# Five of eleven down-projection groups of a decoder layer as bare FP4 codes in two passes, with the running sum rescaled on VectorE

## The chip, the cores and the metric

The kernel runs on one core of one Trainium2 chip. The metric is the time of the program on the device in microseconds (us), as the median of several runs. The core has five engines that run side by side and meet only through semaphores: TensorE (matrix products, PE in the profile, its weight loads PEld), VectorE (DVE), ScalarE (ACT), GpSimd (POOL) and SyncE (SP), which here issues every DMA. Each engine works off its own instructions in order: an instruction that waits holds up all behind it on that engine.

## What is computed

x and ctx are 8 x 256 x 512 in fp32. Three stages, each followed by a layer norm with a residual:

```
x  = LN(x + attention(x))            # linear attention with a memory, head width 128
x  = LN(x + conv(ctx, ctx, x))       # 32 heads of 8: outer products of ctx, causal convolution, times x
x  = LN(x + ffn(x))

def ffn(x):
    w_gu   = FP4_LUT[gate_up codes] * scale    # [2816, 512], a scale for each row and group of 128 inputs
    w_down = FP4_LUT[down codes] * scale       # [512, 1408], 11 groups of 128 inputs, down_scales [11, 512]
    gate, up = split(x @ w_gu.T)
    y = (silu(gate) * up) @ w_down.T
    return y / sqrt(mean(y * y) + 1e-6)
```

## The kernel before

**Stages.** The attention works in 8 slots of 256 tokens; its results x1 go to DRAM in two layouts (x1_rows by token, x1_blocks for the transposed reads). Then come 8 groups g of 256 tokens for convolution and FFN. They are pipelined in passes: pass g does the convolution of group g (c0 to c15 on TensorE, tm0 to tm15 on VectorE, tr0 to tr3 on GpSimd) and the FFN of group f = g - 1. The attention, the unpacking of the weights and pass 1 (its steps bear a "+") share one written-out order, the start. Passes 2 to 7 follow one order (PE_ORDER and its sisters); 3 to 6 are a loop; in pass 7 the steps of the next group are left out. Pass 8 has only FFN (LAST_PE and its sisters). The steps kq, ct, kn, ln, d0 and d1 in a pass belong to the next group. The half t = 1 of the down projection of group f (y1_i) is done in the pass after that of its half t = 0 (y0_i); in the last pass the half t = 1 of the last group is called w1_i.

**What sets the order.** For each engine, an order of step names is written out by hand in the text, and every step waits on semaphores for what it needs. No step moves by itself.

**Gate and up.** w_gu is kept as bare FP4 codes, exact in fp16, for each group of 128 inputs k = 0 to 3. gi_p is phase p of hidden tile i: four matmuls of 256 columns (x2_hi and x2_lo, gate and up) into one bank of p_gu. Between the phases ScalarE multiplies the running sum in place by a ratio of scales (rsi_p, line 1134). Silu (gu on ScalarE), the product (gu on VectorE, line 1201), h_hi (hhi, ScalarE, line 1151) and h_lo (hli, GpSimd, line 1102) follow.

**Down.** y0_i, y1_i and w1_i are down(f, t, i), lines 1290 to 1304. The weight of group i is scaled in fp32 and split into wd_hi + wd_lo in fp16; a step has three matmuls of 512 columns with accumulation over all eleven groups in one PSUM bank p_y[t]: h_hi by wd_hi (line 1297), h_hi by wd_lo (1298), h_lo by wd_hi (1299). Then a square sum (n0, n1 on ScalarE), a mean (a), a root on GpSimd (a, b), the residual z with its statistics (b, line 1216) and the norm to fin (e, line 1232), which SyncE stores. Capitals (A1, B1, E1, N1) are the same steps of the last group's half 1.

**The weights in the start.** Tiles n = 0 to 21 are gate/up, 22 to 32 down. wsn (GpSimd) lays out bytes or multiplies a down tile by its scale, wn (TensorE) flips it, by one 128-column flip for a gate/up tile and four for a down tile; whn (ScalarE) makes the fp16 high part and wln (VectorE, line 795) the low part of the down tiles. u0 to u4 (VectorE) unpack the codes.

**Other steps named below.** Xa, Xb: flips of x; Q, V, S, M, N, T, Oa, Ob: attention products on TensorE; dn, lc, o: denominators, local part and sum of attention; qs, bn, pw, nb, nm: statistics and norm of x1 (nm, ScalarE, line 631). On SyncE, stn stores x1 of slot n (one DMA at line 410, eight at line 415), xn loads x, cx ctx, tw writes the Toeplitz rows, toe reads them, xq and xr read x1_blocks and x1_rows. In the convolution kq (VectorE, line 223) transposes xq, hk and kl/lk/ln split the pair products (pr, pn on GpSimd) into kv_hi (line 180) and kv_lo (line 216), f and ct flip ctx, rt and xt flip the sum and x2; bs, bn, nm and the xt of VectorE (line 285) end in x2_lo, for which the first gate step g0_0 of the next pass waits.

The step on TensorE that changes:

```python
def down(f, t, i):
    ...
    pe.wait_ge(h_low, f * GI + i + 1)
    nc.tensor.matmul(p_y[t][:], h_hi[:, i, c], wd_hi[:, i, :], start=(i == 0), stop=False)
    nc.tensor.matmul(p_y[t][:], h_hi[:, i, c], wd_lo[:, i, :], start=False, stop=False)
    done = nc.tensor.matmul(p_y[t][:], h_lo[:, i, c], wd_hi[:, i, :], start=False, stop=(i == GI - 1))
```

## Time and profile before

| | |
|---|---|
| runs | 536.75, 536.4, 536.91 us; median 536.75 |
| profiled execution: span from first to last instruction | 535.3 us (it has no other time of its own) |
| TensorE busy | 508.7 us, 95% |
| ScalarE | 415.7 us, 78% |
| GpSimd | 394.7 us, 74% |
| VectorE | 374.4 us, 70% |
| mean granted TensorE clock | 0.995 of full |
| DMA | 40.63 MB, mean 76 GB/s |

The start with pass 1 ends at about 180 us; passes 2 to 6 take some 51.2 us each, pass 7 some 46; pass 8 begins near 482. Busy times of TensorE are modelled and overlap (a 512-column matmul is listed with 0.38 us though the next begins 0.22 us later), so its cost is read from one start to the next. A line of the timeline gives the start in us, the duration, the engine, the line of the kernel, the operation, output <- input with their shapes and a count; in square brackets stands the idle time of the engine before it and what ended it.

### The profile page before, as it was taken

Reading aid. Unit: us, or ns where it says so; the run is one execution under the profiler, and the core shown is the slowest. Engines: PE = TensorE matmul, PEld = TensorE weight load, DVE = VectorE, ACT = ScalarE, POOL = GpSimd, SP = SyncE. Lnnn points to the kernel's source line nnn. Section 1 sums busy time; section 2 is a strip of 40 time slices with the busy share of each in tenths; the row PEclk is TensorE's granted clock in tenths of the full one; section 3 lists DMA queues with packets and bytes.
Section 4 is the critical chain, followed back from the end, with each engine's and each line's share of the span. In section 5 each row is a group of like instructions: output and inputs, shape, how many; then the busy total and the mean of one; then the engine's idle time right before and its main releaser. Section 6 shows DMA issues by size and latency. Waiting matters only on the chain.

```text
span 535.3 us, 11768 instructions
## 1 busy us (share of the span) xinstructions
PE 508.7 (95%) x3676; PEld 377.6 (71%) x3676; DVE 374.4 (70%) x1145; ACT 415.7 (78%) x994; POOL 394.7 (74%) x449
## 2 busy tenths in 40 slices
PE   8888899998999999999999999999999999999992
PEld 5676787777785777677767776777677767765660
DVE  2886668988787667776777776768777777763223
ACT  4577875277999788788888897889788877788981
POOL 2768864994898499769968995899589859871231
PEclk9999999999999999999999999999999999999997
DMA  8713776443250862032104210411040111001001
GB/s 224 203 39 63 169 142 180 128 80 99 87 112 24 159 127 86 23 100 79 60 1 117 59 59 0 118 59 59 13 130 14 39 33 49 0 1 42 1 21 39
DMA packets 66146, 40.63 MB, mean 76 GB/s; under 512 B 37882, under 2 KB 55418, under 8 KB 66106
## 3 DMA queue, kind: packets, MB, share of 16 engines
q1 hardware_dynamic: 66106, 40.13, 29.6%
q8 instruction: 20, 0.33, 0.3%
q14 instruction: 20, 0.16, 0.1%
HBM read 27.46 MB, written 12.66 MB: 75 GB/s over the span
## 4 chain that ended last, share of the span: by engine, by line
PE 36%; POOL 27%; issue 19%; ACT 5%; DVE 4%; SPq 4%; DMA 2%; POOLq 1%; DVEq 0%; ACTq 0%
POOL shared L297 9%; POOL h_lo L1102 5%; SPq L415 4%; POOL kv L197 3%; PE p_cv L137 3%; PE p_cv L139 3%; PE p_cv L138 3%; PE p_n L1299 3%; PE p_n L1297 3%; PE p_n L1298 3%; POOL shared L299 2%; PE p_x L1284 2%; PE p_x L1286 2%; PE p_qk L1284 2%; PE p_qk L1286 2%
## 5 line engine op out<-in xcount | busy, mean ns | idle before, releaser
L1102 POOL TENSOR_TENSOR h_lo<-w,h_hi 128x256 f16<-128x256 f32 x88 | 73.6, 842 | 44.6 <-ACT h_hi L1151 43.0
L137 PE MATMUL p_cv<-kv_hi,toe 128*128 128x288 f16 x320 | 91.6, 286 | 1.3 <-DVE shared L257 1.3
L139 PE MATMUL p_cv<-kv_hi,toe 128*128 128x288 f16 x320 | 91.5, 286 | 0.0
L138 PE MATMUL p_cv<-kv_lo,toe 128*128 128x288 f16 x320 | 91.5, 286 | 0.0
L1134 ACT ACTIVATE p_qk<-p_qk,rescale 128x256 f32<-128x256 f32 x192 | 78.3, 451 | 12.5 <-PE p_qk L1286 11.9
L297 POOL TENSOR_TENSOR shared<-shared 128x1024 f32<-128x1024 f32 x32 | 76.8, 2399 | 8.9 <-DVE shared L257 8.8
L1134 ACT ACTIVATE p_x<-p_x,rescale 128x256 f32<-128x256 f32 x192 | 78.4, 452 | 6.2 <-PE p_x L1286 6.0
L1134 ACT ACTIVATE p_s<-p_s,rescale 128x256 f32<-128x256 f32 x144 | 59.0, 456 | 11.2 <-PE p_s L1286 11.1
L1297 PE MATMUL p_n<-wd_hi,h_hi 128*128 128x512 f16 x176 | 66.8, 379 | 0.0
L1298 PE MATMUL p_n<-wd_lo,h_hi 128*128 128x512 f16 x176 | 66.7, 379 | 0.0
L1299 PE MATMUL p_n<-wd_hi,h_lo 128*128 128x512 f16 x176 | 66.7, 379 | 0.0
L1284 PE MATMUL p_qk<-x_hi,wg_hi 128*128 128x256 f16 x256 | 63.0, 273 | 3.6 <-DVE x_lo L285 2.1
L1284 PE MATMUL p_x<-x_hi,wg_hi 128*128 128x256 f16 x256 | 62.9, 273 | 0.7 <-ACT p_x L1134 0.2
L1286 PE MATMUL p_x<-x_lo,wg_hi 128*128 128x256 f16 x256 | 62.8, 273 | 0.0
L1286 PE MATMUL p_qk<-x_lo,wg_hi 128*128 128x256 f16 x256 | 62.8, 273 | 0.0
L239 DVE TENSOR_TENSOR shared<-p_cv,qv 128x128 f32<-128x128 f32 x128 | 36.1, 282 | 32.4 <-PE p_cv L139 31.8
L216 DVE TENSOR_TENSOR kv_lo<-kv,kv_hi 128x1152 f16<-128x1152 f32 x32 | 52.6, 1642 | 3.4 <-ACT kv_hi L180 3.4
L242 DVE TENSOR_TENSOR shared<-p_cv,qv 128x128 f32<-128x128 f32 x128 | 49.7, 388 | 0.0
L299 POOL TENSOR_TENSOR shared<-shared 128x512 f32<-128x512 f32 x32 | 47.7, 1492 | 2.5
L1284 PE MATMUL p_s<-x_hi,wg_hi 128*128 128x256 f16 x192 | 47.1, 273 | 0.9 <-ACT p_s L1134 0.9
L1286 PE MATMUL p_s<-x_lo,wg_hi 128*128 128x256 f16 x192 | 47.1, 273 | 0.0
L180 ACT CAST kv_hi<-kv 128x1152 f16<-128x1152 f32 x32 | 37.3, 1166 | 10.9 <-POOL kv L208 7.2
(170 smaller groups left out, 1270.6 us busy)
## 6 DMA issues: line engine op xcount, KB each, us to landing
toe<-toeplitz_rows SPq DMA_DIRECT2D x16, 512.0 KB, 4.0
cnat<-in_ctx SPq DMA_DIRECT2D x16, 256.0 KB
xq<-x_blocks SPq DMA_DIRECT2D x16, 256.0 KB, 5.7
xr<-x_rows SPq DMA_DIRECT2D x16, 256.0 KB
out_x<-fin SPq DMA_DIRECT2D x16, 256.0 KB
ring<-in_x SPq DMA_DIRECT2D x6, 512.0 KB, 4.4
x_rows<-ring SPq DMA_DIRECT2D x6, 512.0 KB, 2.9
x_blocks<-ring SPq DMA_DIRECT2D x48, 64.0 KB
```

Of the source, the lines that this page charges most:

```text
L137: nc.tensor.matmul(dst, hi, kh, start=(mb == 0), stop=False)
L138: nc.tensor.matmul(dst, hi, kl, start=False, stop=False)
L139: done = nc.tensor.matmul(dst, lo, kh, start=False, stop=(mb == lb))
L297: nc.gpsimd.tensor_tensor(T[:, :, 0:256], T[:, :, 0:256], T[:, :, 256:512], ALU.add).then_inc(cv.tree, 1)
L299: nc.gpsimd.tensor_tensor(T[:, :, 0:128], T[:, :, 0:128], T[:, :, 128:256], ALU.add).then_inc(cv.tree, 1)
L1102: nc.gpsimd.tensor_tensor(h_lo[:, i, :], h32[:, i % 2, :], h_hi[:, i, :], ALU.subtract).then_inc(h_low, 1)
L1134: done = nc.scalar.activation(sums, sums, ACT.Copy, scale=rescale[:, p - 1, part * GI + i:part * GI + i + 1])
L1284: nc.tensor.matmul(dst, whi, cv.x2_hi[:, k, :], start=(k == 0 and part == 0), stop=False, skip_group_check=True)
L1286: done = nc.tensor.matmul(dst, whi, cv.x2_lo[:, k, :], start=False, stop=True, skip_group_check=True)
L1297: nc.tensor.matmul(p_y[t][:], h_hi[:, i, c], wd_hi[:, i, :], start=(i == 0), stop=False)
L1298: nc.tensor.matmul(p_y[t][:], h_hi[:, i, c], wd_lo[:, i, :], start=False, stop=False)
L1299: done = nc.tensor.matmul(p_y[t][:], h_lo[:, i, c], wd_hi[:, i, :], start=False, stop=(i == GI - 1))
```

## The change

EX = 5: the down groups 0 to 4 are kept as bare codes. Their weight tiles are laid out and flipped as gate/up tiles are, there is no wd_lo for them, and down(f, t, i) has two matmuls for i < 5. After each of them VectorE multiplies the running sum in the bank by the ratio of the scales of group i and group i + 1, a row of 512 numbers (rescale_down, steps s0_i, s1_i and, for the last half, S1_i); y_(i+1) waits for that. The remaining weights enter with their scales as before. The bank's ratio of group 4 is the scale itself, since group 5 is not a bare code.

The ratios are made once: SyncE loads the scales of five groups onto 16 partitions, VectorE forms ratios (dr0, five small operations), rw0 stores them to DRAM in runs of 128 bytes, and rl0 loads them onto all 128 partitions (five rows of 2 KB for each, 1.31 MB). The tensor early, which receives them, holds pk_d, kin, kpad and the fp32 scale rows until then. high_h waits for the last reader of its h_hi by another semaphore. deviations (ScalarE) and add_residual (VectorE) get a wait on their own engine's earlier work. All sequences are new.

```diff
+EX = 5
...
+    early = keep["early"]
+    srow_gf = early[0:KD * OG, 1856:1984]
+    srow_df = early[0:GI * 4, 1984:2112]
...
+        sp.dma_start(dn_rows[:], dn_scales[0:EX].rearrange("g (p c) -> p g c", c=32)).then_inc(in_dr, 16)
...
+            elif name == "rw":
+                sp.wait_ge(ratios_made, 5)
+                sp.dma_start(ratio_rows.rearrange("g (p c) -> p g c", c=32), dn_abs[:]).then_inc(ratios_stored, 16)
+            elif name == "rl":
+                sp.wait_ge(ratios_stored, 16)
+                sp.wait_ge(scales_flipped, 2)
+                sp.wait_ge(unpacked, 30)
+                sp.wait_ge(rows_stored, 16)
+                sp.dma_start(early[:, 0:EX * D].rearrange("p (g d) -> p g d", g=EX), bass.AP(ratio_rows.tensor, 0, [[0, P], [D, EX], [1, D]])).then_inc(
+                    keep["in_ratio"], 16)
...
-                if kind == "g":
+                if kind == "g" or idx < EX:
                     out = w32[:, n % 2, 0:P].bitcast(U8).rearrange("p (c h g) -> p h g c", h=2, g=4)
-                    src = vg.bitcast(U8)[:, idx * 256:(idx + 1) * 256].rearrange("p (g c) -> p g c", g=4)
+                    if kind == "g":
+                        src = vg.bitcast(U8)[:, idx * 256:(idx + 1) * 256].rearrange("p (g c) -> p g c", g=4)
+                    else:
+                        src = vd.bitcast(U8).rearrange("p (t g c) -> p g t c", t=4, g=GI)[:, idx]
...
+            elif idx < EX:
+                dst = keep["wd_hi"][:, idx, :].rearrange("p (t c) -> p t c", t=4)
+                src = wbank[n % 2][:, 0:P].bitcast(F8).rearrange("p (c t) -> p t c", t=4)
...
+            wait(act, deviated, 2 * i)
...
+        def down_ratios():
+
+            dve.wait_ge(in_dr, 16)
+            nc.vector.tensor_scalar(dn_abs[:], dn_rows[:], FP4_SHIFT, None, ALU.mult).then_inc(ratios_made, 1)
+            dve.wait_ge(ratios_made, 1)
+            nc.vector.tensor_scalar(dn_rec[:], dn_abs[:], 0.0, NO_SCALE, ALU.is_equal, ALU.mult).then_inc(
+                ratios_made, 1)
+            dve.wait_ge(ratios_made, 2)
+            nc.vector.tensor_tensor(dn_abs[:], dn_abs[:], dn_rec[:], ALU.add).then_inc(ratios_made, 1)
+            dve.wait_ge(ratios_made, 3)
+            nc.vector.reciprocal(dn_rec[:, 1:EX], dn_abs[:, 1:EX]).then_inc(ratios_made, 1)
+            dve.wait_ge(ratios_made, 4)
+            nc.vector.tensor_tensor(dn_abs[:, 0:EX - 1], dn_abs[:, 0:EX - 1], dn_rec[:, 1:EX], ALU.mult).then_inc(
+                ratios_made, 1)
+
...
-            for g in range(1 if n < OG else 4):
+                pe.wait_ge(w_low, n - 2 - OG - EX + 1)
+            for g in range(1 if n < OG + EX else 4):
...
-            if i < GI - 1:
-                wait(act, h_spent, (f - 1) * (GI - 1) + i + 1)
+            if i < EX:
+                wait(act, y_part[1], (f - 1) * EX + i + 1)
+            elif i < GI - 1:
+                wait(act, h_spent, (f - 1) * (GI - 1 - EX) + i - EX + 1)
...
+        def rescale_down(f, t, i):
+            dve.wait_ge(y_part[t], f * EX + i + 1)
+            if isinstance(f, int) and f == 0 and t == 0 and i == 0:
+                dve.wait_ge(keep["in_ratio"], 16)
+            nc.vector.tensor_tensor(p_y[t][:], p_y[t][:], keep["early"][:, i * D:(i + 1) * D], ALU.mult).then_inc(y_rescaled[t], 1)
...
+            wait(dve, fin_made[t], f)
...
+            if 0 < i <= EX:
+                pe.wait_ge(y_rescaled[t], f * EX + i)
+            nc.tensor.matmul(p_y[t][:], h_hi[:, i, c], wd_hi[:, i, :], start=(i == 0), stop=False,
+                             skip_group_check=True)
+            if i >= EX:
+                nc.tensor.matmul(p_y[t][:], h_hi[:, i, c], wd_lo[:, i - EX, :], start=False, stop=False,
+                                 skip_group_check=True)
+            done = nc.tensor.matmul(p_y[t][:], h_lo[:, i, c], wd_hi[:, i, :], start=False,
+                                    stop=(i < EX or i == GI - 1), skip_group_check=True)
+            if i < EX:
+                done.then_inc(y_part[t], 1)
...
-    START_SYNC = ("x3 x4 cx2 st0 cx3 tw0 x5 st1 st2 x6 st3 toe0 xq0 xq2 toe1 xq1 x7 cx5 cx4 xr1 xr0 toe2 st4 cx6 xq3 "
-                  "xr2 toe3 xq5 xr3 st5 toe4 xq4 cx7 st6 toe5 st7").split()
+    START_SYNC = ("x3 tw0 cx2 x4 cx3 rw0 toe0 toe1 st0 x5 st1 st2 x6 st3 rl0 xr1 xq0 cx4 xr0 xq1 x7 cx5 xq2 "
+                  "xq3 toe3 toe2 xq5 xr2 xq4 xr3 toe4 st4 cx7 toe5 cx6 st5 st6 st7").split()
-    START_DVE = ("ze0 is0 u0 sg0 mk0 ig0 dn0 fs0 o0 u1 sg1 ra0 rb0 bm0 mk1 u2 dn1 bn0 o1 kl0 nb0 sg2 ra1 rb1 bm1 mk2 "
...
-                 "wl23 o4 wl24 wl25 wl26 ra4 rb4 wl27 sg5 bm4 wl28 mk5 wl29 wl30 dn5 bn4 wl31 o5 wl32 kq0 tm0 tm1 sg6 "
-                 "tm2 tm3 nb4 tm4 kl2 tm5 kq1 tm6 ra5 tm7 rb5 tm8 mk6 tm9 kl3 tm10 tm11 dn6 tm12 tm13 o6 tm14 tm15 bm5 "
...
+    START_DVE = ("ze0 is0 sg0 ig0 mk0 u0 dn0 o0 u1 sg1 ra0 rb0 bm0 mk1 u2 dn1 bn0 o1 sk0 ra1 sg2 rb1 bm1 mk2 "
...
+                 "mk4 nb3 dn4 o4 kl0 ra4 rb4 sg5 wl27 wl28 wl29 wl30 mk5 wl31 wl32 bm4 kq0 dn5 kl1 tm0 tm1 "
+                 "tm2 o5 tm3 tm4 kq1 tm5 kl2 tm6 sg6 ra5 tm7 tm8 rb5 tm9 tm10 kq2 kl3 mk6 tm11 bm5 tm12 tm13 "
...
-    START_ACT = ("xa0 kw0 kw1 xb0 kw2 kw3 re0 ge0 vk0 ks0 xa1 xb1 lc0 rv0 wh0 wh1 re1 ok0 kt0 wh2 rv1 wh3 qs0 xa2 vk1 "
-                 "xb2 wh4 hk0 wh5 lc1 re2 ok1 wh6 nm0 wh7 wh8 qs1 xa3 vk2 xb3 wh9 hk1 lc2 wh10 ok2 wh11 re3 wh12 wh13 "
-                 "qs2 xa4 vk3 wh14 xb4 nm1 lc3 wh15 wh16 wh17 wh18 ok3 nm2 wh19 re4 wh20 qs3 vk4 wh21 xa5 wh22 xb5 nm3 "
...
+    START_ACT = ("xa0 xb0 kw0 kw1 kw2 kw3 re0 ge0 vk0 xa1 xb1 lc0 ks0 ok0 re1 wh0 wh1 rv0 wh2 wh3 rv1 kt0 "
+                 "xa2 vk1 qs0 xb2 kt1 wh4 wh5 lc1 ok1 re2 wh6 wh7 wh8 wh9 hk0 xa3 vk2 wh10 xb3 wh11 qs1 lc2 "
+                 "rv2 nm0 ok2 re3 wh12 wh13 wh14 wh15 qs2 xa4 vk3 wh16 xb4 nm1 lc3 wh17 wh18 ok3 re4 wh19 "
...
-    START_PE = ("ze0 Xa0 iw0 iw1 iw2 Xb0 iw3 Q0 iz0 V0 S0 Xa1 M0 N0 Xb1 w0 w1 Q1 T0 w2 f0 w3 Oa0 Ob0 Xa2 S1 V1 w4 w5 "
...
-                "Xb4 w15 M3 N3 w16 Q4 w17 T3 w18 f1 Oa3 w19 Ob3 w20 w21 Xa5 V4 S4 M4 w22 w23 Xb5 N4 w24 Q5 T4 w25 w26 "
-                "Oa4 Ob4 w27 w28 Xa6 V5 w29 S5 w30 Xb6 M5 N5 w31 w32 Q6 c0 c1 c2 c3 c4 f2 T5 Oa5 c5 S6 c6 c7 c8 Ob5 "
-                "f3 c9 Xa7 V6 c10 c11 M6 N6 Xb7 c12 rt0 c13 c14 c15 T6 Q7 Oa6 Ob6 +c0 +c1 rt1 S7 V7 xt0 M7 N7 xt1 "
...
+    START_PE = ("ze0 Xa0 Xb0 iw0 iw1 iw2 iw3 Q0 V0 S0 Xa1 M0 N0 Xb1 iz0 Q1 T0 w0 w1 Xa2 Oa0 Ob0 w2 S1 f0 w3 "
...
+                "w13 Oa2 Ob2 w14 w15 V3 S3 w16 w17 Xb4 M3 N3 w18 Q4 T3 f2 w19 w20 Oa3 Ob3 w21 Xa5 V4 S4 w22 "
+                "Xb5 M4 N4 w23 w24 Q5 T4 w25 w26 Oa4 Ob4 w27 w28 V5 w29 w30 Xa6 S5 w31 M5 w32 N5 Xb6 c0 c1 "
+                "Q6 c2 c3 c4 Xa7 T5 c5 c6 Oa5 f3 c7 c8 Ob5 S6 c9 c10 V6 c11 c12 M6 N6 c13 Xb7 c14 c15 rt0 T6 "
...
-    PE_ORDER = ("y1_0 g0_0 g1_0 y1_1 g0_1 y1_2 ct0 g1_1 g0_2 y1_3 y1_4 g2_0 g0_3 c2 g1_2 g3_0 c3 y1_5 g2_1 g1_3 g3_1 "
-                "c4 g2_2 c5 y1_6 g4_0 g2_3 c6 g3_2 c7 g4_1 g5_0 y1_7 g3_3 c8 g5_1 c9 y1_8 g4_2 y1_9 g5_2 c10 g6_0 "
-                "y1_10 c11 g4_3 g6_1 g5_3 ct1 c12 g7_0 g6_2 c13 c14 g8_0 g7_1 c15 y0_0 g7_2 g8_1 g6_3 rt0 y0_1 g7_3 "
-                "g8_2 y0_2 g9_0 y0_3 g10_0 g8_3 g9_1 y0_4 g10_1 g9_2 d0 rt1 y0_5 g10_2 g9_3 y0_6 d1 g10_3 xt0 y0_7 "
-                "y0_8 y0_9 xt1 y0_10").split()
+    PE_ORDER = ("g0_0 g1_0 y1_0 g2_0 g0_1 ct0 g1_1 g2_1 g0_2 g1_2 g0_3 y1_1 g1_3 c2 g3_0 c3 g3_1 g4_0 y1_2 "
+                "g2_2 c4 g3_2 g4_1 c5 g2_3 c6 y1_3 c7 g5_0 y1_4 y0_0 g3_3 g5_1 y1_5 g4_2 ct1 c8 g5_2 y1_6 "
+                "y1_7 g4_3 y1_8 y1_9 g6_0 y1_10 c9 c10 g5_3 g7_0 c11 c12 g6_1 g7_1 c13 g8_0 g6_2 g7_2 c14 "
+                "c15 g8_1 y0_1 g6_3 g7_3 g8_2 y0_2 rt0 g9_0 g10_0 y0_3 g8_3 g9_1 g10_1 y0_4 rt1 g9_2 g10_2 "
+                "y0_5 g9_3 g10_3 xt0 y0_6 y0_7 y0_8 xt1 y0_9 y0_10 d0 d1").split()
-    DVE_ORDER = ("tm0 tm1 gu0 lk1 tm2 tm3 gu1 tm4 tm5 gu2 lk2 tm6 tm7 tm8 gu3 tm9 tm10 lk3 tm11 gu4 a1 tm12 gu5 tm13 "
-                 "kq0 tm14 tm15 b1 gu6 gu7 ln kq1 bs0 bn0 bs1 bn1 gu8 nm0 gu9 nm1 gu10 xt0 xt1 a0 b0 e1 e0").split()
+    DVE_ORDER = ("s1_0 tm0 gu0 tm1 lk1 gu1 s1_1 tm2 tm3 s1_2 tm4 tm5 s1_3 gu2 lk2 s1_4 tm6 tm7 tm8 gu3 lk3 "
+                 "gu4 a1 tm9 tm10 s0_0 gu5 tm11 tm12 tm13 b1 tm14 tm15 s0_1 gu6 gu7 s0_2 bs0 s0_3 bn0 s0_4 "
+                 "bs1 nm0 gu8 bn1 gu9 gu10 xt0 nm1 ln xt1 e1 a0 b0 kq0 kq1 e0").split()
-    LAST_PE = ("y1_0 y1_1 y1_2 g0_0 g1_0 g2_0 g0_1 g1_1 y1_3 y1_4 g0_2 g2_1 g1_2 y1_5 g0_3 g2_2 g1_3 y1_6 g3_0 g2_3 "
-               "g4_0 g3_1 y1_7 g5_0 y1_8 g4_1 y1_9 g3_2 y0_0 g5_1 g4_2 y1_10 g3_3 g5_2 y0_1 g4_3 y0_2 g6_0 g5_3 g6_1 "
-               "g7_0 y0_3 g6_2 g8_0 g7_1 g6_3 y0_4 g7_2 w1_0 g8_1 g9_0 w1_1 g7_3 y0_5 w1_2 g10_0 g8_2 w1_3 g9_1 "
-               "g10_1 g8_3 g9_2 w1_4 g10_2 w1_5 g9_3 w1_6 g10_3 w1_7 y0_6 w1_8 w1_9 w1_10 y0_7 y0_8 y0_9 y0_10").split()
+    LAST_PE = ("g0_0 g1_0 g2_0 y1_0 g0_1 g1_1 g2_1 g0_2 g1_2 g2_2 y1_1 g0_3 g1_3 g2_3 y1_2 g3_0 g4_0 y1_3 "
+               "g3_1 y0_0 g4_1 y1_4 g5_0 g3_2 g4_2 y1_5 y1_6 g5_1 g3_3 g4_3 y1_7 y1_8 g6_0 g7_0 y1_9 y1_10 "
+               "g6_1 g7_1 y0_1 g5_2 g6_2 g7_2 w1_0 g5_3 g6_3 g7_3 y0_2 w1_1 g8_0 g9_0 y0_3 w1_2 g10_0 g8_1 "
+               "g9_1 w1_3 g10_1 y0_4 g8_2 w1_4 g9_2 g10_2 g8_3 w1_5 g9_3 w1_6 g10_3 y0_5 w1_7 w1_8 w1_9 "
+               "w1_10 y0_6 y0_7 y0_8 y0_9 y0_10").split()
-    LAST_DVE = ("gu0 gu1 gu2 a1 gu3 gu4 gu5 b1 gu6 gu7 gu8 e1 gu9 gu10 A1 B1 a0 b0 E1 e0").split()
+    LAST_DVE = ("s1_0 s1_1 gu0 gu1 s1_2 s1_3 gu2 s1_4 s0_0 gu3 gu4 a1 s0_1 b1 S1_0 gu5 gu6 s0_2 S1_1 gu7 "
+                "S1_2 s0_3 S1_3 S1_4 e1 s0_4 gu8 gu9 gu10 A1 B1 a0 b0 E1 e0").split()
...
```

## Rows read from the trace of the kernel before

**Rows 1.** Windows view: window, its length, busy us (xcount) per engine, PEclk.
```profile
119.50:180.00 60.50, 57.27 (x434) 42.83 (x435) 47.69 (x142) 54.07 (x129) 44.51 (x49) 1.00 0.37 84
...
282.30:333.50 51.20, 51.02 (x389) 37.71 (x387) 38.47 (x122) 42.89 (x105) 42.90 (x46) 1.00 0.22 61
...
482.00:510.00 28.00, 26.66 (x187) 17.54 (x186) 8.95 (x20) 25.41 (x71) 5.66 (x9) 1.00 0.07 20
```

**Rows 2.** Waits of the pass 282.3 to 333.5: total us, times, longest.
```profile
DVE shared L239 <- PE p_cv L139: 4.5, 5, 1.4
...
PE p_qk L1284 <- DVE x_lo L285: 0.2, 1, 0.2
```

**Rows 3.** The chain that ended last, shares by engine (page).
```profile
PE 36%; POOL 27%; issue 19%; ACT 5%; DVE 4%; SPq 4%; DMA 2%; POOLq 1%; DVEq 0%; ACTq 0%
```

**Rows 4.** Timeline of TensorE, pass 4: start, us, instruction.
```profile
320.16 0.38 PE L1297 MATMUL p_n<-wd_hi,h_hi 128*128 128x512 f16 x1
...
320.81 0.27 PE L1284 MATMUL p_x<-x_hi,wg_hi 128*128 128x256 f16 x1
...
321.68 0.29 PE L137 MATMUL p_cv<-kv_hi,toe 128*128 128x288 f16 x1
...
322.05 0.60 PE L102 MATMUL p_ct<-ident,shared 128*128 128x128 f32 x4
322.49 0.38 PE L1297 MATMUL p_n<-wd_hi,h_hi 128*128 128x512 f16 x1
```

**Rows 5.** Groups by line, VectorE: busy us, mean ns, idle before.
```profile
L285 DVE TENSOR_TENSOR x_lo<-p_ct,x_hi 128x512 f16<-128x512 f32 x16 | 11.0, 690 | 12.8 <-ACT x_hi L184 12.7
...
L265 DVE TENSOR_TENSOR shared<-p_ct,xr 128x512 f32<-128x512 f32 x16 | 10.7, 671 | 4.5 <-PE p_ct L102 4.5
```

**Rows 6.** Timelines of VectorE and GpSimd in the same pass.
```profile
287.00 1.36 DVE L216 TENSOR_TENSOR kv_lo<-kv,kv_hi 128x1152 f16<-128x1152 f32 x1 [0.58 <-ACT kv_hi L180]
...
327.31 0.69 DVE L285 TENSOR_TENSOR x_lo<-p_ct,x_hi 128x512 f16<-128x512 f32 x1 [0.22 <-ACT x_hi L184]
...
287.36 1.54 POOL L1102 TENSOR_TENSOR h_lo<-w,h_hi 128x256 f16<-128x256 f32 x1 [1.64 <-ACT h_hi L1151]
...
326.87 1.46 POOL L1102 TENSOR_TENSOR h_lo<-w,h_hi 128x256 f16<-128x256 f32 x2 [0.45 <-ACT h_hi L1151]
```

**Rows 7.** Timelines at the pass boundary: TensorE once, then VectorE.
```profile
328.25 0.60 PE L102 MATMUL p_ct<-ident,shared 128*128 128x128 f32 x4
...
282.92 1.40 DVE L1232 TENSOR_SCALAR fin<-z,mv,rs 128x512 f32<-128x512 f32 x1 [0.53 <-POOL rs L1098]
...
329.51 0.69 DVE L285 TENSOR_TENSOR x_lo<-p_ct,x_hi 128x512 f16<-128x512 f32 x1 [1.50 <-ACT x_hi L184]
...
331.07 0.75 DVE L1216 SCALAR_TENSOR_TENSOR z<-p_n,rr,x2hold 128x512 f32<-128x512 f32 x1 [0.66 <-POOL rr L1098]
...
332.93 0.15 DVE L1224 TENSOR_SCALAR ve<-mv 128x1 f32<-128x1 f32 x1
```

**Rows 8.** Timelines in the start: VectorE (kq0), TensorE (c2).
```profile
87.06 0.71 DVE L223 STREAM_TRANSPOSE qv<-xq 128x512 f32<-128x512 f32 x1 [1.14 <-DMA xq<-x_blocks]
...
88.92 0.30 PE L137 MATMUL p_cv<-kv_hi,toe 128*128 128x288 f16 x1 [0.65 <-DVE shared L257]
```

**Rows 9.** Timelines in the start: DMA issues of SyncE, then ScalarE (lc2).
```profile
38.37 7.19 SPq L415 DMA_DIRECT2D x_blocks<-ring  x8
...
56.44 0.38 SPq L410 DMA_DIRECT2D x_rows<-ring  x1
...
72.21 8.19 SPq L415 DMA_DIRECT2D x_blocks<-z  x8
...
83.34 4.90 SPq L426 DMA_DIRECT2D xq<-x_blocks  x2
...
44.94 0.64 ACT L600 ACTIVATE loc<-p_n,coef 128x128 f32<-128x128 f32 x2
```

**Rows 10.** DMA view, 78 to 92 us: GB/s in 40 equal slices.
```profile
GB/s 86 87 87 85 86 84 88 87 82 75 89 106 302 246 222 252 249 184 67 173 294 174 23 20 6 0 0 0 0 0 0 91 94 328 356 376 380 348 301 244
```

More of the change, by code:

```diff
@@ L811, in step @@
                 factor_scales()
+            elif name == "dr":
+                down_ratios()
             elif name == "sk":
@@ L1037, in periods @@
         "y_done", "y_squared", "y_used", "rr_made", "rs3_made", "fin_made", "y_steps"))
+    y_part, y_rescaled = ([sem(f"{n}{t}") for t in range(GT)] for n in ("y_part", "y_rescaled"))
     def before(i):
@@ L1296, in down @@
             pe.wait_ge(h_low, f * GI + i + 1)
[L1297 to L1300 removed]
+            if 0 < i <= EX:
[9 more added lines that the diff above has]
+                done.then_inc(y_part[t], 1)
+            elif i == GI - 1:
                 done.then_inc(y_done[t], 1)
@@ new lines, in decoder_layer @@
+    START_SYNC = ("x3 tw0 cx2 x4 cx3 rw0 toe0 toe1 st0 x5 st1 st2 x6 st3 rl0 xr1 xq0 cx4 xr0 xq1 x7 cx5 xq2 "
+                  "xq3 toe3 toe2 xq5 xr2 xq4 xr3 toe4 st4 cx7 toe5 cx6 st5 st6 st7").split()
+    START_PE = ("ze0 Xa0 Xb0 iw0 iw1 iw2 iw3 Q0 V0 S0 Xa1 M0 N0 Xb1 iz0 Q1 T0 w0 w1 Xa2 Oa0 Ob0 w2 S1 f0 w3 "
[9 rows of a table added]
+                "+y0_6 +y0_7 +y0_8 +y0_9 +xt1 +y0_10 +d0 +d1").split()
+    START_DVE = ("ze0 is0 sg0 ig0 mk0 u0 dn0 o0 u1 sg1 ra0 rb0 bm0 mk1 u2 dn1 bn0 o1 sk0 ra1 sg2 rb1 bm1 mk2 "
[7 rows of a table added]
+                 "+kq0 +b0 +kq1 +e0").split()
@@ new lines, in decoder_layer @@
+    ACT_ORDER = ("rv0 rs0_1 rs1_1 rs2_1 rs0_2 rs1_2 rs0_3 rs1_3 tl gu0 hk1 gu1 hh0 rs3_1 rs2_2 rs3_2 rs4_1 "
+                 "hh1 rs2_3 hk2 rs4_2 rs3_3 ct0 gu2 rs5_1 rv1 rs5_2 gu3 hh2 rs4_3 hh3 hk3 gu4 ho0 rs5_3 n1 "
+                 "rs6_1 hh4 gu5 rs7_1 rs6_2 hh5 rs7_2 rs8_1 ct1 rs6_3 rs7_3 ho1 rs8_2 gu6 gu7 hh6 rs8_3 hh7 "
+                 "rs9_1 rs10_1 gu8 rs9_2 rs10_2 rs9_3 rs10_3 hh8 gu9 gu10 xt0 hh9 hh10 kn xt1 n0").split()
+    POOL_ORDER = ("pr1 pr2 hl0 hl1 tr0 pr3 hl2 tr1 hl3 pn a1 hl4 hl5 tr2 tr3 bn0 hl6 b1 hl7 hl8 bn1 hl9 hl10 "
+                  "a0 b0").split()
```

61 lines of the change are left out of this document (28 added, 33 removed), and 36 rows, old and new, of tables (START_ACT, START_DVE, START_PE, START_POOL).

## The prediction

> **What bounds the kernel now.** I read the windows view first. In a steady pass of 51.20 us TensorE is busy 51.02 us, ScalarE 42.89, GpSimd 42.90, VectorE 38.47, at full granted clock [rows 1]. The waits of that pass agree: TensorE waits only 0.2 us, for the low half of x2, while VectorE waits 4.5 us for convolution sums [rows 2]. The chain of waits credits GpSimd with 27% [rows 3], but a step followed back through an engine that sits idle in between is no proof that it binds; here TensorE has no gap. What a pass costs is its matmuls' start-to-start time: three of 512 columns take 0.65 us (0.217 each), one gate/up step 0.44, three of 288 columns 0.37, four flips of 128 columns 0.44 [rows 4]. Ahead of pass 2 TensorE is less full: it idles 3.2 of 60.5 us from 119.5 to 180 [rows 1], and the start waits for memory once (below). In the last pass TensorE is busy 26.66 and ScalarE 25.41 of 28 us: both nearly bind [rows 1].
>
> **What is removed.** 8 FFN passes x 2 token halves x 5 groups = 80 matmuls of 512 columns: 80 x 0.217 = 17.3 us of TensorE. They are spread as 5 in pass 1 (only y0), 10 in each of passes 2 to 7, 15 in the last (y1, y0, w1). Weights 22 to 26 need one flip instead of four: 15 x 0.11 = 1.65 us of TensorE in the start, and five residuals of 0.69 us on VectorE go (the shape of L285) [rows 4, 5].
>
> **What is added on VectorE.** 80 multiplies of a 128x512 PSUM bank by SBUF ratios. The nearest rows are L265 (671 ns) and L285 (690 ns), both PSUM with SBUF [rows 5]. No row writes PSUM from VectorE; I take 0.67, bounds 0.6 and 0.9. Ten a pass make 6.7 us: VectorE rises to 45.2 of a pass that could be 51.2 - 2.17 = 49.0 us, so its unfilled time must shrink from 12.7 to 3.8 us. GpSimd: when both inputs of a VectorE operation lie in SBUF the two exclude each other: the h_lo at 287.36 takes 1.54 us beside L216, but two beside L285 (PSUM and SBUF) take 1.46 together [rows 6]. So I charge the multiplies nothing on GpSimd; were they to hold it up by all of their 6.7 us, GpSimd would need 42.9 + 6.7 = 49.6 us, above 49.0. The Trainium skill's "SBUF — State Buffer", in its section on the two separate sides, says the pair of ports is an exclusive lock, taken by VectorE operations with two SBUF inputs against GpSimd operations that read SBUF. By that page too the new multiply, with one SBUF input, takes no lock; by the trace's lock row alone 49.6 us would have stood.
>
> **The new chain.** y_i, multiply, y_(i+1) is serial: a multiply (0.67) plus two hand-overs, about 0.9 us. In the steady orders the links of y0_1 to y0_5 have 1.3 us of other TensorE work between, so they hold if VectorE is free. The weak link is at the pass boundary. Call X the end of the second x_lo. Before: X = 329.51 + 0.69 = 330.20, z starts 0.87 later, ve ends 2.9 later (332.93 + 0.15), and the second fin takes 1.40 us beside GpSimd's pair products [rows 7]. The new VectorE order is xt1, e1, a0, b0, kq0, kq1, e0, then s1_0. e1 delays a0 by 0.5, so ve ends at X + 3.4; two transposes of 0.7 [rows 8] bring X + 4.7; e0 (0.7, as the other 128x512 operations, to 1.4) and s1_0 (0.67) give X + 6.1 to 6.8. On TensorE y0_9, y0_10 (1.3) and d0, d1 (1.1) follow the flips xt1. Before, x_lo ended 1.95 us after those flips began (328.25) [rows 7]; now ln stands before it, so 1.95 to 2.4. TensorE reaches g0_0 at 0.44 + 2.4 = 2.84 after the flips began: X + 0.4 to 0.9. From there to y1_1 its order holds nine gate steps (4.0), y1_0 (0.43) and ct0 (0.44): 4.8 us. y1_1 wants to start at X + 5.2 to 5.7 and may at X + 6.1 to 6.8: 0.4 to 1.6 us of stall; I take 1.2, since e0 again meets the pair products. Net of the 2.17 us removed: 1.0 us gained a pass (bounds 0.4 and 1.9), six passes: -6.0. The new self-waits (ScalarE's on deviated, VectorE's on fin_made) stand behind work long done in order: nothing; if they cost, 0.2 us at 8 and 16 places.
>
> **The start.** SyncE's queue. Before, st0 issues from 38.37 (7.19 us), st1 from 56.44, st3's blocks from 72.21 (8.19 us), and xq0 at 83.34 once they landed [rows 9]. kq0 waits 1.14 us for it and TensorE reaches c2 at 88.92 after 0.65 us [rows 8]. Two things delay xq0. First, nm0, which releases st0, now stands behind lc2 on ScalarE; that ran at 44.94 [rows 9], so st0 issues at about 47 instead of 38, ends near 55, and x5, which waits for its landing (3 us), holds back st1 to about 58.5: +0 to +2.3. Second, rl0 (128 x 10 KB = 1.31 MB) and xr1 (0.26 MB) are issued before xq0. The transfers of that stretch peaked at 380 GB/s and ran at about 250 with toe0 [rows 10]: 1.57 MB are 4.1 to 6.3 us, of which toe0 (0.52 MB, 2.1 us), now loaded early, is given back: +0 to +4.2, less where st3 is waited for. I take 90.5 for kq0 (87.1 to 93.5). Behind kq0 in VectorE's order stand dn5, kl1 (1.36, its shape in [rows 6]) and only then tm0: c2 at about 94.0 against 88.92, +5.1. The 1.65 us of flips vanish in that wait; c0, c1 moved ahead of Q6 only fill it. Given back behind it: 5 matmuls (1.1), the context flip f2 that moved ahead (0.4), and of the 3.2 us idle [rows 1] I take 1.5. Start: +2.1 (bounds -2.7, no wait, and +5.5). The Trainium skill, "DMA: Bandwidth & Descriptors", section "Queues, rings and completion order", says that an engine consumes the descriptors of one queue in ring order; by it xq0 cannot pass rl0, and the upper bound of +4.2 would hold. No row here shows two such loads queued.
>
> **The last pass.** 15 x 0.217 = 3.25 us less on TensorE. ScalarE's rescales stay; it starts some 2 us earlier, since three gate steps now lead, but g10_3 soon waits for it, and s1_0, s1_1 precede gu0. I take -2.0 (bounds -1.0 and -3.3).
>
> **Sum.** 2.1 - 6.0 - 2.0 = -5.9. The profiled span is 535.3, the median of the three runs 536.75 (the profiled execution has no time of its own beside its span): about 1.45 us lie around the span, and I leave them as they are. 536.75 - 5.9 = 530.8 us.
>
> **Rivals.**
> (A) The order hides everything: no stall at the boundary, none in the start: 17.3 + 1.65 off, 517.8 us. For it: the tight boundary of before costs only 0.2 us. Against: the 3.8 us that VectorE has left. Chance 0.17.
> (B) The start alone costs more: xq0 behind rl0 comes 6 us later than I take, with x7 and Xa7 behind it; the passes gain as forecast: 536.8 us. Chance 0.15.
> (C) Slower: VectorE becomes the bound. Its work is 45.2 us; before, it waited 12.7 us a pass in order. As soon as more than 6.0 of these remain, a pass is longer than 51.2. With 7.0 it is 52.2: six passes +6.0, start +2.1, last pass -2.0: 542.9 us. For it: in-order waits for TensorE's double-buffered convolution banks (4.5 us) come from TensorE's order, which the multiplies don't change. Against: TensorE's shorter order makes those inputs come earlier. Chance 0.18.
> A fourth, that the two-pass groups save no matmul time, has no ground: the 0.217 us are per matmul, whatever its operand.
>
> **How the numbers follow.** My forecast, 530.8, has 0.50 with a range of its own of 525 to 535. (A) 0.17, (B) 0.15, (C) 0.18. A tenth left out at each end gives 521 to 540. A measurement tells about 0.2% (1.1 us): faster is below 535.7, slower above 537.8. The forecast and (A) are faster (0.67); (B) straddles: 0.05 faster, 0.06 same, 0.04 slower; (C) slower 0.17, same 0.01. Faster 0.72, same 0.07, slower 0.21.
>
> **What would show it.** Matmuls of 512 columns: 448 instead of 528. A steady pass of 50.2 us (A: 49.0; C: over 51.2). In the boundary, a TensorE wait for the multiply of about 1.2 us, once a pass, ahead of y1_1. Multiplies of 0.67 us; h_lo on GpSimd no longer beside them. kq0 waiting 5 us or more for xq in the start, c2 near 94. Wrong would be: multiplies over 0.9 us, TensorE waits spread over all links (C), or an xq0 that lands before 87 (A).

## The result, and the profile of the changed kernel

The changed kernel takes 539.88 us (median of 6 runs, 537.92 to 541.01) against 536.83 (median of 6, 536.40 to 537.69) for the kernel before: a ratio of 1.0051, with a 95% interval of 1.0034 to 1.0069. It is slower by about 0.5%. The forecast was 530.8; the time lies just inside the range's upper end of 540, on the wrong side of zero. The profiled execution of the changed kernel took 537.92 us, with a span of 536.2; its other runs lie up to 3.1 us above it, and I come back to that.

First the three windows that answer to [rows 1] and to a stretch of the start: the start behind the first query blocks, a steady pass, the last pass (window, length, busy us per engine in the order TensorE, weight loads, VectorE, ScalarE, GpSimd, then the granted clock, the DMA share and GB/s).

```profile
90.00:120.00 30.00, 21.97 (x158) 16.93 (x159) 23.05 (x94) 7.28 (x13) 19.03 (x19) 0.83 0.33 88
...
284.86:335.48 50.62, 50.07 (x378) 36.20 (x376) 42.54 (x131) 42.66 (x106) 40.82 (x46) 1.00 0.21 62
482.00:510.00 28.00, 27.00 (x181) 16.15 (x180) 14.79 (x30) 24.97 (x69) 7.18 (x12) 1.00 0.08 20
```

Two things are to be seen. A steady pass is 50.62 us, 0.58 shorter than the 51.20 of [rows 1], although 2.17 us of matmuls left it. And from 90 to 120 TensorE is busy 22 of 30 us, at a granted clock of 0.83. The same stretch of the kernel before:

```profile
90.00:120.00 30.00, 28.56 (x202) 22.04 (x201) 26.88 (x100) 14.04 (x25) 26.63 (x22) 1.00 0.51 134
```

The waits behind it stand in the timelines of VectorE and TensorE. These rows answer to [rows 8], and then come the next convolutions (start, us, instruction, idle before and its releaser).

```profile
94.58 0.71 DVE L224 STREAM_TRANSPOSE qv<-xq 128x512 f32<-128x512 f32 x1 [10.73 <-DMA xq<-x_blocks]
...
95.73 1.35 DVE L217 TENSOR_TENSOR kv_lo<-kv,kv_hi 128x1152 f16<-128x1152 f32 x1
97.00 0.28 DVE L240 TENSOR_TENSOR shared<-p_cv,qv 128x128 f32<-128x128 f32 x1
```
```profile
98.00 0.42 PE L138 MATMUL p_cv<-kv_hi,toe 128*128 128x288 f16 x1 [9.71 <-DVE shared L258]
98.22 0.45 PE L139 MATMUL p_cv<-kv_lo,toe 128*128 128x288 f16 x1
...
101.46 0.29 PE L138 MATMUL p_cv<-kv_hi,toe 128*128 128x288 f16 x1
101.58 0.29 PE L139 MATMUL p_cv<-kv_lo,toe 128*128 128x288 f16 x1
```

kq0 starts 7.5 us later than before, c2 9.1 us later, and from c2 to 101.4 the 288-column matmuls follow one another every 0.24 us, afterwards every 0.12. TensorE had idled 9.7 us, and its clock stood at the lower of its two levels (1.2 GHz) when it came back. SyncE's issues answer to [rows 9]:

```profile
48.11 6.55 SPq L421 DMA_DIRECT2D x_blocks<-ring  x8
...
57.87 0.47 SPq L416 DMA_DIRECT2D x_rows<-ring  x1
...
75.46 8.40 SPq L421 DMA_DIRECT2D x_blocks<-z  x8
84.04 0.60 SPq L478 DMA_DIRECT2D early<-ratio_rows  x1
85.24 0.66 SPq L436 DMA_DIRECT2D xr<-x_rows  x1
86.66 0.39 SPq L432 DMA_DIRECT2D xq<-x_blocks  x1
```

xq0 is issued at 86.66 instead of 83.34 (+3.3 us) and kq0 starts 7.92 us after that issue instead of 3.72 (+4.2). kl1 (1.35 us) and the denominators now stand between kq0 and tm0: from kq0 to c2 it is 3.42 us instead of 1.86 (+1.6). 3.3 + 4.2 + 1.6 = 9.1.

A ledger of the two profiled executions needs points that mean the same in both. I take the start of a pass as its first gate matmul, less the down matmuls ahead of it in the order (one y1 of 0.65 us in a steady pass of the kernel before, three in its last, none in the changed kernel).

| stretch | before | after | difference | forecast |
|---|---|---|---|---|
| start with pass 1 | 176.10 | 183.81 | +7.71 | +2.1 |
| passes 2 to 7 | 305.81 | 302.05 | -3.76 | -6.0 |
| last pass, to the end of the span | 53.39 | 50.34 | -3.05 | -2.0 |
| sum, the span | 535.30 | 536.20 | +0.90 | -5.9 |

Counted like this, pass 7 of the kernel before takes 49.9 us, not the 46 named ahead of the prediction, and the start ends at 176.1, not at 180.

The start can be split at c2. It comes 9.1 us later. From c2 to pass 2 the changed kernel needs 1.4 us less (85.8 instead of 87.2), although 3.4 us of that stretch ran at half the rate, which costs some 1.7. So 1.7 + 1.4 = 3.1 us were given back there, as the forecast has it (3.0 in its sum); how this divides among its three parts was not measured.

### The profile page after: what moved, and what is told of

It reads as the page before. It is cut to its first block, busy times and chain, and to the rows that moved or that the text cites. A ratio compares the mean times of both kernels' runs of the same rounds, so it can differ in the third digit from the quotient of the medians.

```text
span 536.2 us, 11775 instructions
## 1 busy us (share of the span) xinstructions
PE 501.7 (94%) x3581; PEld 364.4 (68%) x3581; DVE 407.9 (76%) x1225; ACT 412.5 (77%) x994; POOL 377.5 (70%) x449
## 4 chain that ended last, share of the span: by engine, by line
PE 30%; POOL 24%; issue 16%; ACT 13%; DVE 7%; SPq 6%; DMA 3%; POOLq 1%; ACTq 0%; DVEq 0%
POOL shared L298 7%; SPq L421 5%; POOL h_lo L1145 4%; ACT p_x L1177 3%; PE p_cv L138 3%; ACT p_qk L1177 3%; PE p_cv L139 3%; PE p_cv L140 3%; PE p_n L1353 3%; PE p_n L1358 3%; POOL kv L198 2%; POOL kv L203 2%; POOL shared L305 2%; ACT p_s L1177 2%; PE p_n L1356 2%
## 5 line engine op out<-in xcount | busy, mean ns | idle before, releaser
L1177 ACT ACTIVATE p_qk<-p_qk,rescale 128x256 f32<-128x256 f32 x192 | 81.8, 487 | 17.1 <-PE p_qk L1340 16.9
L1177 ACT ACTIVATE p_x<-p_x,rescale 128x256 f32<-128x256 f32 x192 | 82.4, 495 | 0.0
L1145 POOL TENSOR_TENSOR h_lo<-w,h_hi 128x256 f16<-128x256 f32 x88 | 59.7, 690 | 28.3 <-ACT h_hi L1196 28.1
L298 POOL TENSOR_TENSOR shared<-shared 128x1024 f32<-128x1024 f32 x32 | 75.6, 2364 | 4.8 <-DVE shared L258 4.8
L1177 ACT ACTIVATE p_s<-p_s,rescale 128x256 f32<-128x256 f32 x144 | 60.9, 482 | 14.1 <-PE p_s L1340 14.1
L1254 DVE TENSOR_TENSOR p_n<-p_n,early 128x512 f32<-128x512 f32 x80 | 55.1, 692 | 15.9 <-PE p_n L1358 15.9
L198 POOL TENSOR_TENSOR kv<-kT 128x512 f32<-128x512 f32 x32 | 41.1, 1284 | 32.9 <-DVE kv_lo L217 32.9
L217 DVE TENSOR_TENSOR kv_lo<-kv,kv_hi 128x1152 f16<-128x1152 f32 x32 | 45.9, 1434 | 12.1 <-ACT kv_hi L181 12.1
L544 POOL COPY w<-shared 128x256 uint8<-128x256 uint8 x54 | 35.3, 803 | 25.8 <-DVE shared L767 14.3
```

Of the source, the lines that this page charges most:

```text
L198: ops.tensor_tensor(flat[:, 0:4].rearrange("p i (r j) -> p i r j", j=4), kb[:, :, 0:4].rearrange("p r (i a) -> p i r a", a=1).to_broadcast ...
L298: nc.gpsimd.tensor_tensor(T[:, :, 0:256], T[:, :, 0:256], T[:, :, 256:512], ALU.add).then_inc(cv.tree, 1)
L1145: nc.gpsimd.tensor_tensor(h_lo[:, i, :], h32[:, i % 2, :], h_hi[:, i, :], ALU.subtract).then_inc(h_low, 1)
L1177: done = nc.scalar.activation(sums, sums, ACT.Copy, scale=rescale[:, p - 1, part * GI + i:part * GI + i + 1])
L1254: nc.vector.tensor_tensor(p_y[t][:], p_y[t][:], keep["early"][:, i * D:(i + 1) * D], ALU.mult).then_inc(y_rescaled[t], 1)
```

## The experiments

Theory A for the start: the 1.31 MB of ratio rows, issued ahead of xq0, lengthen its transfer, the late stores delay its issue, and the wait costs a second time through the clock. Its rivals name one of these alone. For the passes: ScalarE's rescales of the gate sums, no longer covered by down work, against the multiplies on VectorE. Every kernel has its ratio to the kernel before, run beside it, whose median lay at 536.83 beside the changed kernel and at 537.07 to 537.25 beside the others; a difference of medians between kernels run apart is thus good to some 0.4 us only.

### The ratio load in the changed kernel, and in the kernel before

```diff
-... st1 st2 x6 st3 rl0 xr1 xq0 cx4 xr0 xq1 x7 cx5 xq2 xq3 toe3 ...
+... st1 st2 x6 st3 xr1 xq0 cx4 xr0 xq1 x7 cx5 xq2 xq3 rl0 toe3 ...
```

> Against the changed kernel one thing moves: the load of the ratio rows (1.31 MB written, L478) is issued behind the fourth load of query blocks, no longer ahead of the first. Theory A (the ring: what is issued ahead of the first block load lengthens it, 7.90 us from issue to landing against 3.70 in the kernel before): the wait ahead of the first transposition (L224) falls from 10.73 to about 6.5 us, that row starts at about 90.4 instead of 94.58, the first convolution that waits for terms at about 93.8 instead of 98.00, and the time falls by about 4 us, to about 535.8. Rival B (the late stores of normalised blocks alone make the load late): the wait stays over 10 us and the time within 1 us of the changed kernel.

Measured: 534.98 us (12 runs), ratio to the kernel before 0.9967 (0.9954 to 0.9981); against the changed kernel's 539.88, -4.9 us (-4.5 by the ratios). Rows of this kernel, VectorE and TensorE:

```profile
91.36 0.71 DVE L224 STREAM_TRANSPOSE qv<-xq 128x512 f32<-128x512 f32 x1 [5.68 <-DMA xq<-x_blocks]
...
94.78 0.30 PE L138 MATMUL p_cv<-kv_hi,toe 128*128 128x288 f16 x1 [4.66 <-DVE shared L258]
```

In this kernel xq0 was issued at 88.23 and kq0 follows 3.13 us later, not 7.92. Theory A holds. TensorE still waits 4.66 us, and the granted clock from 90 to 120 is 0.94 instead of 0.83, so a part of the gain is the clock's. The counter-test puts such a load into the kernel before, where nothing else is late. It writes the memory of h_hi and h_lo, whose first writer waits for it (that part of the edit is left out here):

```diff
+            elif name == "bl":
+                sp.dma_start(keep["hh"][:, 0:NB * D].rearrange("p (g d) -> p g d", g=NB),
+                             bass.AP(x.tensor, 0, [[0, P], [D, NB], [1, D]])).then_inc(keep["in_hh"], 16)
-... st1 st2 x6 st3 toe0 xq0 xq2 ...
+... st1 st2 x6 st3 toe0 bl0 xq0 xq2 ...
```

> The kernel before, with one thing of the change added: a broadcast load of the size of the ratio rows (5 rows of 512 floats to 128 partitions, 1.31 MB), of data nobody uses, issued right ahead of the first block load. Theory A (the ring): the block load takes 7 to 8 us to land instead of 3.70, the wait ahead of the first transposition is 5 us or more instead of 1.14, the first waiting convolution starts at 93 instead of 88.92, and the kernel before becomes slower by 4 to 6 us (541 to 543). Rival B (the ratio load only matters in the changed kernel, whose stores are late): under 1 us.

Measured: 542.77 us, ratio 1.0103 (1.0088 to 1.0118), +5.5 us.

```profile
83.26 9.21 SPq L427 DMA_DIRECT2D xq<-x_blocks  x2
...
91.30 0.71 DVE L224 STREAM_TRANSPOSE qv<-xq 128x512 f32<-128x512 f32 x1 [5.35 <-DMA xq<-x_blocks]
```
```profile
90.00:120.00 30.00, 26.15 (x181) 20.13 (x182) 24.06 (x98) 8.50 (x14) 20.29 (x17) 0.89 0.43 115
```

The first fence is SyncE's and VectorE's timeline of this kernel, the second its windows view. The issue is where it was (83.26, [rows 9]), kq0 comes 8.04 us later instead of 3.72, and c2 starts at 93.15, 4.2 us late. The clock falls here too, to 0.89. One load in the wrong place costs a tuned kernel 1%. By the Trainium skill, "DMA: Bandwidth & Descriptors", section "Queues, rings and completion order", an engine takes the descriptors of one queue in ring order. The landings agree: in both kernels xq0, a fifth of the size and issued 2.6 and 2.1 us behind the large load, landed after it (the large load 7.3 us behind its issue at 84.04 in the changed kernel, 9.3 us behind 81.18 in this one).

### The stores ahead of it

```diff
-START_POOL ... ws9 ws10 ws11 ws12 pw0 ws13 ws14 ws15 ws16 ws17 pw1 ...
+START_POOL ... ws9 pw0 ws10 ws11 ws12 ws13 ws14 pw1 ws15 ws16 ws17 ...
-START_DVE ... sk0 ra1 ... dr0 dn2 nb0 o2 u3 ra2 rb2 bm2 sg3 bn1 nb1 ...
+START_DVE ... sk0 nb0 ra1 ... dr0 dn2 bn1 o2 u3 nb1 ra2 rb2 bm2 sg3 ...
-START_ACT ... wh7 ... rv2 nm0 ok2 re3 wh12 ... xb4 nm1 lc3 wh17 wh18 ok3 re4 wh19 wh20 nm2 ...
+START_ACT ... wh7 nm0 ... rv2 ok2 re3 wh12 nm1 ... xb4 lc3 nm2 wh17 wh18 ok3 re4 wh19 wh20 ...
```

> Against the changed kernel only the chain of the first layer norms moves forward on VectorE, ScalarE and GpSimd (root, shift and normalisation of row blocks 0 to 2); the ratio rows stay ahead of the block load. Theory A (two causes, which add): the fourth set of stores ends at about 80 instead of 83.86, the block load is issued at about 83 instead of 86.66 and lands 7 to 8 us later, the transposition starts at about 91 instead of 94.58, time about 536.5. Rival B (only the ring counts): nothing falls. Rival C (the stores are bound by their own issue on SyncE, some 8 us each, so an earlier first one frees the later ones by less than half): a gain of 1 us or less.

Measured: 540.23 us, ratio 1.0054 (1.0041 to 1.0067): nothing gained, as rivals B and C both allow. The timelines of ScalarE and SyncE say why:

```profile
51.16 1.52 ACT L655 ACTIVATE ring<-ring,shift,rs 128x512 f32<-128x512 f32 x2
```
```profile
44.65 0.35 SPq L472 DMA_DIRECT2D ratio_rows<-dn_abs  x1
...
46.09 1.14 SPq L416 DMA_DIRECT2D x_rows<-ring  x1
...
58.05 0.37 SPq L412 DMA_DIRECT2D ring<-in_x  x1
58.46 0.47 SPq L416 DMA_DIRECT2D x_rows<-ring  x1
```

Row block 1 is normalised at 52.7, but its stores start at 58.46: x5 stands ahead of them on SyncE and waits for st0's landing. The new store rw0 (44.65) holds st0, whose rows are ready at 40.6, in the same way. In the changed kernel itself the norm does end last ahead of st0 (47.64, the store at 47.67); with the norm early, the queue's order takes its place. Next, all three start edits at once (the two above, and `kq0` behind `dn5 kl1` on VectorE):

> The edits of the two kernels ahead of this one together, and on VectorE the 1.35 us kv_lo subtraction and the denominators stand ahead of the first transposition, not behind it. If the three causes add (4.2 us ring, 3.3 us stores, 1.6 us VectorE order): the transposition starts at about 87, the first convolution waiting for terms at about 89, as in the kernel before (88.92), TensorE's granted clock doesn't fall behind that wait, and the time is about 529.5. Rival (the gain is met by the next wait, such as the ratio rows or the third and fourth block load): over 533.

Measured: 535.31 us, ratio 0.9971 (0.9954 to 0.9988), against the 529.5 of the sum, and no better than the ratio load's move alone (534.98). This is the rival's result: TensorE waits 2.57 us ahead of c2, and 1.80 us at 97.01 for the next block of x. In the profile the VectorE order gives what it should (kq0 at 90.24, c2 at 92.10: 1.86 us apart again), but xq0 is issued at 87.37. So SyncE's order was changed too:

```diff
-... rw0 toe0 toe1 st0 x5 st1 st2 x6 st3 xr1 xq0 ...
+... st0 rw0 toe0 toe1 st1 x5 st2 x6 st3 xr1 xq0 ...
```

> The kernel with all three start edits, and in addition SyncE's own order: the first stores go ahead of the ratio rows' store and the Toeplitz loads, and the load of row block 5 goes behind the second stores, which it held up (the second stores started at 58.8 us although their rows were ready at about 50). Theory A (the stores were held by SyncE's order, not by the norms): the first stores start at about 40, the second at 50 to 52, the block load is issued near 83 instead of 87.4, TensorE reaches the first convolution that waits for terms at 88 to 90 instead of 92.10, and the time falls by about 3 us against that kernel, to about 532.5. Rival B (the stores are held by the DMA ring: 24 to 26 us for four sets wherever they start): the load stays at 86 to 88 us and the time within 1 us.

Measured: 529.79 us, ratio 0.9852 (0.9839 to 0.9865): 5.5 us below the kernel ahead of it and 7.4 below the kernel before, run beside it. The profiled executions of the two kernels differ by 1.6 us only (529.3 and 530.9); this one had lost 1.8 us in its first 9 us, which I come back to, so they show some 3.4 us for the queue's order, and the rest lies in the scatter of both (2.9 and 5.4 us). The order was changed on top of the early norms and never alone. TensorE's wait is gone, though c2 isn't early:

```profile
93.02 0.30 PE L138 MATMUL p_cv<-kv_hi,toe 128*128 128x288 f16 x1 [0.26 <-DVE shared L258]
```

The time of c2 is thus a poor measure by itself: here TensorE has no hole ahead of it and the clock stays 1.00 from 90 to 120. My own edit had opened another hole at 42 us (VectorE waits 2.92 us for GpSimd's root, TensorE 2.32 us for the split queued behind it). Closing it, with `pw0` behind `ws7`:

> The kernel with SyncE's order repaired, and GpSimd's first root two weight tiles earlier. In that kernel VectorE waited 2.92 us for this root with a residual and a query split queued behind, and TensorE 2.32 us for the split, at the granted clock 0.90 and 0.76 in the stretches 40 to 45 and 45 to 50. If that was the cost of the early norm: both waits fall under 0.5 us, the first convolution that waits for terms comes at about 90.5 instead of 93.0, the time falls by 2 to 3 us to about 527.5. Rival (TensorE then waits for the blocks at 91 anyway): under 1 us.

Measured: 530.71 us, ratio 0.9877 (0.9862 to 0.9892): no gain. The wait at 42 us is gone, and a new one stands on TensorE at 67, for x5, which the previous edit had put behind st1 (its issue comes at 62.31):

```profile
67.17 0.92 PE L899 MATMUL p_x<-ident,ring 128*128 128x128 f32 x4 [4.00 <-DMA ring<-in_x]
```

The rival's result, by another load than the one it named.

### What the clock adds

```diff
+        def keep_warm(n):
+            pe.wait_ge(masked, 6)
+            pe.wait_ge(oT_kept, 5)
+            for k in range(n):
+                nc.tensor.matmul(p_s[:], keep["wg_hi"][:, 0, 0:P], keep["wg_hi"][:, 0, 0:512], start=True, stop=True)
...
+                if i == 2:
+                    keep_warm(40)
```

> Against the changed kernel, 40 matmuls of 512 columns (8.7 us at 0.217 us each) whose sums nobody uses are put on TensorE ahead of the first convolution that waits for terms, inside its 9.7 us wait. Theory A (the wait costs twice: by itself, and by the lower granted clock behind it, 0.83 in the stretch 90 to 120, with 288-column matmuls 0.24 us apart instead of 0.12): the granted clock of that stretch is 1.00, the time falls by 1.7 to 3 us to 537 to 538, and the runs, which lay 3.1 us apart, come within about 1.5 us of each other. Rival B (the lower clock costs nothing, since later waits absorb it): no change. Rival C (the extra work itself delays the transposition or the start of the convolution): slower.

Measured: 537.44 us (11 runs, 536.88 to 539.56), ratio 1.0014 (1.0004 to 1.0025): 2.4 us less than the changed kernel by the medians, 2.0 by the ratios (1.0051 and 1.0014), with 40 matmuls more. From c2 (98.95) to pass 2 (183.09) it is 84.1 us instead of 85.8, 1.7 less.

```profile
90.00:120.00 30.00, 28.35 (x197) 19.91 (x196) 23.71 (x98) 7.90 (x15) 19.68 (x19) 1.00 0.36 95
```

The mean granted clock of its runs is 0.993 to 0.996, as in the kernel before (0.993 to 0.996), against 0.980 to 0.986 in the changed kernel. So the lower clock cost about 2 us beyond the wait. The second half of theory A fell: the runs still lie 2.7 us apart (1.4 us in the kernel before).

### Inside a steady pass

TensorE's start-to-start times, less the nominal time of each matmul, give 1.86 us of gaps in the pass that starts at 284.86. Three of them stand in the first 5 us, at the gate steps g0_2, g1_2 and g0_3 (0.20, 0.28, 0.34 us), four more at later gate steps (0.25, 0.19, 0.07, 0.06), 0.42 at the flips of x2 and at d0. The kernel before has some 0.4 from 279.13 to 330.33, nearly all of it ahead of the first gate matmul, for x2_lo ([rows 2]). ScalarE's and TensorE's timelines at the head:

```profile
287.65 0.85 ACT L1177 ACTIVATE p_qk<-p_qk,rescale 128x256 f32<-128x256 f32 x2
288.36 0.86 ACT L1177 ACTIVATE p_x<-p_x,rescale 128x256 f32<-128x256 f32 x2
289.20 0.81 ACT L1177 ACTIVATE p_qk<-p_qk,rescale 128x256 f32<-128x256 f32 x2
```
```profile
289.28 0.28 PE L1338 MATMUL p_x<-x_hi,wg_hi 128*128 128x256 f16 x1
...
290.07 0.28 PE L1338 MATMUL p_qk<-x_hi,wg_hi 128*128 128x256 f16 x1 [0.18 <-ACT p_qk L1177]
```

ScalarE works without a break, one pair every 0.73 us, while a gate step takes TensorE 0.44. y1_1, ahead of which I had forecast the stall, starts at 290.51 without waiting: VectorE's multiply ran at 289.43. Two kernels shrink one side each. Both leave a part of the scaling out, so their results are not the function's:

```diff
-            nc.vector.tensor_tensor(p_y[t][:], p_y[t][:], keep["early"][:, i * D:(i + 1) * D], ALU.mult)...
+            nc.vector.tensor_tensor(p_y[t][:, 0:16], p_y[t][:, 0:16], keep["early"][:, i * D:i * D + 16], ALU.mult)...
```

> The multiplies by the ratio rows take only the first 16 of 512 columns (the other columns go unscaled: part of the computation is left out); instructions, waits and order stay. Theory A (a steady pass of 50.6 us holds about 1.7 us of TensorE idle behind ScalarE's rescaling of the gate groups at its head, because less down work stands between them; the multiplies cost nothing): the pass stays at 50.3 to 50.6 us and the time falls by under 2 us. Rival B (VectorE's 6.9 us of multiplies a pass are what holds the pass): the pass falls to about 49.2 us and the time by 8 to 10 us.

Measured: 540.07 us, ratio 1.0064 (1.0046 to 1.0083); the multiplies took 176 ns each instead of 692.

```profile
285.26:336.12 50.86, 50.07 (x378) 36.21 (x376) 37.97 (x131) 42.76 (x106) 40.77 (x46) 1.00 0.21 62
```

With 4.6 us less of VectorE's work in it (37.97 against 42.54) the pass is no shorter, but 0.24 longer, which I can't explain. VectorE doesn't hold it.

```diff
-                done = nc.scalar.activation(sums, sums, ACT.Copy,
+                done = nc.scalar.activation(sums[:, 0:16], sums[:, 0:16], ACT.Copy,
```

> Against the changed kernel ScalarE's rescaling of the gate sums takes only the first 16 columns of each half (the rest stays unscaled: part of the computation is left out); instructions, waits and order stay, and each pair of activations takes about 0.4 us instead of 0.73. Theory A (what a steady pass loses, 50.63 us against 48.7 of matmuls, is TensorE waiting for these rescales where too little down work stands between the gate groups): the pass falls to 48.9 to 49.3 us, the time by 9 to 12 us. Rival B (the loss is elsewhere: in the multiplies' chain, in GpSimd or in hand-overs): the pass stays over 50 us.

Measured: 531.66 us, ratio 0.9905 (0.9887 to 0.9923), 8.2 us below the changed kernel.

```profile
281.22:331.19 49.97, 49.58 (x379) 36.63 (x377) 42.60 (x131) 31.31 (x106) 40.84 (x46) 1.00 0.22 63
```
```profile
L1177 ACT ACTIVATE p_x<-p_x,rescale 128x16 f32<-128x16 f32 x192 | 40.0, 249 | 5.2 <-PE p_x L1340 4.0
```

The direction is A's, the size isn't: the pass falls to 49.97, by 0.65 us, not by the 1.3 to 1.7 expected. The gaps at the gate steps fall from 1.39 to 0.29 us, but others come up: y1_1 now waits 0.28 us for its multiply, a flip of x2 0.26 that it didn't wait before. The forecast's link exists; ScalarE's rescales lay over it. The profiled span falls by 7.9 us: 2.4 in the start, 4.2 in passes 2 to 7 and 1.3 in the last pass (49.05 instead of 50.34). Last, an order meant to win some of this back:

```diff
-DVE_ORDER ... s0_2 bs0 s0_3 bn0 s0_4 bs1 nm0 ... e1 a0 b0 kq0 kq1 e0
+DVE_ORDER ... s0_2 bs0 kq0 s0_3 bn0 s0_4 bs1 kq1 nm0 ... e1 a0 b0 e0
-PE_ORDER ... g1_2 g0_3 y1_1 g1_3 c2 g3_0 ...
+PE_ORDER ... g1_2 y1_1 g0_3 c2 g1_3 g3_0 ...
```

> Against the changed kernel only the order of the steady passes changes: on VectorE the two transpositions of the next query blocks move from the pass's end, where they stand ahead of the first multiply, to the gap among the mean squares; on TensorE y1_1 and the third convolution move ahead of the last gate groups that wait for ScalarE (g0_3, g1_3). Theory A (TensorE's head of a pass is short of work that doesn't wait for ScalarE; 0.82 us is lost there): one wait of 0.3 us goes, the pass falls from 50.63 to about 50.3, the time by about 2 us to 538. Rival B (ScalarE's seven rescales in a row, 0.73 us each, end where they ended, and the wait only moves): pass 50.6, no change. Rival C (y1_1 now waits for its multiply): slower by up to 2 us.

Measured: 544.63 us, ratio 1.0139 (1.0124 to 1.0155); a pass takes 51.80 us, 1.2 more.

```profile
291.14 1.43 DVE L1284 TENSOR_SCALAR fin<-z,mv,rs 128x512 f32<-128x512 f32 x1 [0.76 <-POOL rs L1141]
292.50 0.68 DVE L1254 TENSOR_TENSOR p_n<-p_n,early 128x512 f32<-128x512 f32 x1
```
```profile
293.24 0.39 PE L1353 MATMUL p_n<-wd_hi,h_hi 128*128 128x512 f16 x1 [0.47 <-DVE p_n L1254]
```

The two transpositions had covered GpSimd's root, for which fin now waits; the multiply is no earlier (4.76 us after the first gate matmul instead of 4.57), so y1_1, moved ahead, waits 0.63 us. The transpositions in their new place delay the statistics of x2, and its flips wait 0.68 us. Rival C, and the link of the forecast laid open.

### The first flips, and all together

The next kernel is the one with GpSimd's root early (530.71 us), with its first flips changed:

```diff
-START_PE ze0 Xa0 Xb0 iw0 iw1 iw2 iw3 ...
+START_PE ze0 Xa0 iw0 iw1 iw2 Xb0 iw3 ...
-START_ACT xa0 xb0 kw0 kw1 kw2 kw3 ...
+START_ACT xa0 kw0 kw1 xb0 kw2 kw3 ...
```

> The kernel of the run ahead, and the first flips on TensorE in the order of the kernel before: the second half of row block 0 behind three projections, not ahead of them, where it waits 0.77 us for ScalarE's copy. In two of the profiles of changed kernels the flips from 4.7 to 9 us took 1.06 us per four and in the others 0.60 to 0.66, and all that followed lay 1.8 us later; in two profiles with the old order the work at 36 us lay within 0.02 us. Theory A (this is part of the spread of the changed kernels' times): the spread of the runs falls under 2 us and the median by about 1 us. Rival B: the spread has another cause and stays.

Measured: 529.58 us (528.52 to 531.14), ratio 0.9869 (0.9854 to 0.9884). The median is 1.1 us below that kernel's, too little for 4 runs each to decide, and the spread is 2.6 us (1.7 there), as rival B has it. The last kernel adds to this one PE_ORDER and DVE_ORDER of the steady order above.

> The kernel of the run ahead with the steady order of the first of these four runs. If the effects add, the time is the sum of their gains: about 524.5 to 525. If the steady order brings nothing, as its rival has it, the time equals that of the run ahead.

Measured: 534.75 us, ratio 0.9959 (0.9945 to 0.9972): 5.2 us above the kernel without them, so the steady order costs in the repaired kernel too.

## Why the prediction was wrong

The step that failed is the start: +7.7 us where I had +2.1 (and at most +5.5), which alone turns the sign. Of the 5.6 us, 4.0 are c2's delay (+9.1 for +5.1), all of it in kq0, since from kq0 to c2 I had 3.5 us and it took 3.4; the rest, about 1.7, is the lower clock, a term that was missing.

- **xq0 behind the ratio rows.** The cause was named, with upper bounds of +2.3 for the issue and +4.2 for the transfer. I took 90.5 for kq0, 3.4 us later than before, about half of the 6.5 that both give together; they measured +3.3 and +4.2, and kq0 started at 94.58, beyond my bound of 93.5. I had no ground to take half: the ring rule stood beside it, and the bound of +4.2, which already gives toe0's 2.1 us back, is what was measured. The load's place costs 5.5 us in the kernel before and 4.5 to 4.9 in the changed one. Rival B, with a chance of 0.15, had this mechanism, with kq0 6 us beyond my 90.5 where it came 4.1 beyond.
- **SyncE's order.** The issue's +3.3 went over my bound of +2.3. I followed st0 and x5 and stopped at st1. It began 1.4 us late, within the bound, but its issues then took 7.97 us where the kernel before needed 6.17 ([rows 9] show only the first and the last set). Why they took longer was not tested. With the norms early, changing the queue's order was worth 5.5 us by the medians.
- **The clock.** It stood nowhere in the sum. A wait of 9.7 us brought TensorE back at 1.2 GHz; the keep-warm kernel prices it at 2.0 to 2.4 us by the medians, and at 1.7 behind c2 in the profiled executions.
- **The steady pass.** -0.58 us each in the loop (passes 2 and 7: -0.8), not -1.0. Removed: 2.17 us, as worked out (448 matmuls of 512 columns are left). The given-back part was 1.6 us instead of 1.2, and its cause was another: ScalarE's rescales, which I had left out since ScalarE is busy 42.9 of 51.2 us in [rows 1]. A share of a whole pass hides a stretch of 5 us in which ScalarE binds. The link through the multiply, my whole argument, cost nothing as long as those waits lay over it, and 0.28 us with the small rescales, not 1.2. I also took y1_1's place in the order as fixed by its matmuls alone and didn't ask which engine paces the nine gate steps ahead of it.
- **The multiplies** take 0.69 us (forecast 0.67), nothing on GpSimd (40.82 us busy a pass, 42.90 before), and VectorE is not the bound: 42.5 us of 50.6, where I had 45.2. Its kv_lo and fin became shorter on average (1.43 us instead of 1.64, 0.72 instead of 0.88), which covers a part of that. Rival C falls with the small multiplies; that the kernel is slower, as it said, has another cause. The Trainium skill's lock rule ("SBUF — State Buffer", the section on the two separate sides) agrees with the trace.
- **The last pass**, -3.1 us, lies near the bound of -3.3, not at -2.0. I had taken off 1.3 us for ScalarE. With the small rescales this stretch is 1.3 us shorter, so ScalarE does hold it; whether it held the kernel before by as much, which would leave nothing to take off, was not tested.
- **The rest.** Of the 9.1 us between forecast and median, 5.6 are the start, 2.2 the passes, -1.1 the last pass, 2.0 the distance of the median from the profiled execution, and 0.3 what lies around its span. The 2.0 are the changed kernel's larger scatter. Part is the clock (its runs' mean granted clocks differ by 0.006, and holding the clock took 2.0 to 2.4 us off the median); the scatter that is left in the keep-warm kernel is not explained. In the profiled executions of two experiments (the ratio load behind, SyncE's order) the first flips (4.7 to 9 us) ran at 1.06 us per four instead of 0.60 to 0.66 and all that followed lay 1.8 us later, but mending their order didn't narrow the runs. What sets it stays open.

The gain that the change does have was paid away in the start: with the same FP4 groups and ratios, but the ratio load behind the query blocks, SyncE's stores nearer to their readiness and VectorE's kv_lo ahead of the first transposition, the kernel takes 529.6 to 529.8 us, 1.3 to 1.5% less than before. Both kernels beat the one before and the changed one; which of the two is better, their runs don't tell.

## What to carry to other kernels

Put a new large load behind every load that someone waits for, and price its place by bytes ahead of the critical one, at the full bound; test it by adding a dummy load of that size to the old kernel. Where a single queue issues stores of 6 to 10 us each, order it by readiness, for one wait ahead holds all behind it. When matmuls are taken from between other steps, look at which engine paces those steps in that stretch of 5 us, not at its share of the pass.

## What the runs showed of the hardware that was not expected

- After 9.7 us of idling TensorE ran 288-column matmuls 0.24 us apart for 3.4 us; with dummy matmuls in 8.7 us of that time the first of them came 0.12 to 0.13 us apart. Work that nobody uses made the kernel faster by about 2 us.
- After idling 2.57 us (the kernel with all three start edits) the window 90 to 120 shows a granted clock of 1.00 in the profiled execution, while the mean clocks of that kernel's runs range from 0.984 to 0.996. A wait of 2.33 us at 40.6 in the same execution left the clock at 1.00 from 40 to 50, and one of 2.32 us at 42.7, at the same step in the kernel with SyncE's order changed, goes with 0.90 from 40 to 45 and 0.76 from 45 to 50. Whether the clock falls at a wait of this length thus differs between executions.
- A VectorE multiply with a PSUM bank as input and output and ratios in SBUF takes 692 ns for 128x512 and 176 ns for 128x16; a ScalarE rescale of a PSUM bank takes 482 to 495 ns for 128x256 and 246 to 249 for 128x16, so that there a sixteenth of the columns costs half the time.
